# Second attention of a two-layer network: scores on one half of TensorE's rows, row maxima on the other, weighings in halves of 256 columns

## The reference, cut to what matters

```
q = (x @ Wq.T + bq).reshape(B, N, H, d)      # B=1, N=2048, H=16, d=8; k and v likewise
q, k = _rope(q, k)
scores = einsum('bhnd,bhmd->bhnm', q, k) / sqrt(d)
attn = softmax(scores, axis=-1)              # over 2048 keys, no mask
out = einsum('bhnm,bhmd->bhnd', attn, v)
return out.reshape(B, N, H*d) @ Wo.T + bo
```

## Time and profile before

| | us |
|---|---|
| median of 3 runs | 1331.21 (1330.64 to 1332.17) |
| the profiled execution | 1332.31 |
| its span | 1330.5 |
| first to last weighing tile of the second attention | 545.38 to 1219.41 of the span |
| TensorE busy | 1273.1 (96%) |
| VectorE busy | 955.4 (72%) |
| ScalarE busy | 861.5 (65%) |

### The profile page before, as it was taken

One profiled execution on the slowest core, in us unless ns is written; L12 is line 12 of the kernel. 1 busy time (PEld: TensorE's weight loads), 2 busy tenths in 40 slices (PEclk: granted clock), 3 DMA queues, 4 the chain that ended last, 5 costly groups with the idle time before them and its releaser, 6 DMA issues. The chain is left out here.

```text
span 1330.5 us, 22445 instructions
## 1 busy us (share of the span) xinstructions
PE 1273.1 (96%) x8134; PEld 729.4 (55%) x8134; DVE 955.4 (72%) x1664; ACT 861.5 (65%) x2406; POOL 189.8 (14%) x369
## 2 busy tenths in 40 slices
PE   5999999999988879999999999999999999999899
PEld 3677777777856643444444444444444444434577
DVE  4566666666667879888988889888888888846300
ACT  2566666666746420677777778777877778786442
POOL 3233333333453130000000000010000000000200
PEclk8999999999998975799999999999999999999899
DMA  2100000000000030000000000000000000000100
GB/s 79 71 10 1 9 10 10 9 1 4 1 1 0 1 148 27 17 20 21 21 22 22 7 16 21 22 16 7 21 21 22 4 19 4 6 5 1 36 17 16
DMA packets 21931, 25.58 MB, mean 19 GB/s; under 512 B 6277, under 2 KB 16293, under 8 KB 20582
## 3 DMA queue, kind: packets, MB, share of 16 engines
q1 hardware_dynamic: 21822, 24.15, 5.9%
HBM read 16.47 MB, written 5.24 MB: 16 GB/s over the span
## 5 line engine op out<-in xcount | busy, mean ns | idle before, releaser
L1206 DVE TENSOR_REDUCE rowmax<-psum 128x1 f32<-128x1024 f32 x512 | 602.8, 1219 | 86.6 <-PE psum L1076 86.4
L1311 ACT ACTIVATE pb<-psum 128x512 f32<-128x512 f32 x1024 | 531.9, 603 | 123.4 <-PE psum L1113 120.5
L1113 PE MATMUL psum<-qf,kf 64*128 64x512 f32 x1024 | 374.1, 441 | 1.6 <-ACT pb L1311 0.9
L1076 PE MATMUL psum<-kf,qf 64*128 64x512 f32 x1024 | 363.3, 454 | 6.3 <-DVE rowmax L1206 3.9
L1113 PEld LDWEIGHTS psum<-qf,kf 64*128 64x128 f32 x1024 | 171.1, 185 | 273.5 <-ACT pb L1311 253.1
L1101 PE MATMUL psum<-pb,vx 128*32 128x512 f32 x2048 | 273.6, 606 | 0.0
L1076 PEld LDWEIGHTS psum<-kf,qf 64*128 64x128 f32 x1024 | 166.4, 195 | 57.4 <-DVE rowmax L1206 31.5
L532 ACT ACTIVATE pr<-psum,nmax 128x128 f32<-128x128 f32 x256 | 93.9, 367 | 113.9 <-DVE nmax L475 113.8
L570 POOL TENSOR_TENSOR pr<-pr,rtotal 128x256 f32<-128x256 f32 (+1 forms) x256 | 110.5, 453 | 239.1 <-DVE rtotal L483 239.1
L474 DVE TENSOR_REDUCE nmax<-psum 128x2 f32<-128x256 f32 x128 | 53.7, 419 | 65.0 <-PE psum L343 65.0
L1345 POOL CAST nparts<-nfull 128x16 fp32r<-128x16 f32 x16 | 3.2, 197 | 665.2 <-DVE nfull L1215 665.2
(11 more groups left out here) (216 smaller groups left out, 1384.9 us busy)
## 6 DMA issues: line engine op xcount, KB each, us to landing
qf<-q_parts SPq DMA_DIRECT2D x30, 128.0 KB
kf<-k_parts SPq DMA_DIRECT2D x30, 128.0 KB
k_parts<-parts SPq DMA_DIRECT2D x4, 512.0 KB, 3.0
q_parts<-parts SPq DMA_DIRECT2D x4, 512.0 KB, 4.2
cos<-cos_table SPq DMA_DIRECT2D x1, 1024.0 KB
sin<-sin_table SPq DMA_DIRECT2D x1, 1024.0 KB
sumsT<-acc SPq DMA_DIRECT2D x60, 16.0 KB
attT<-acc SPq DMA_DIRECT2D x60, 16.0 KB
```

The lines of the kernel that those rows point to most:

```text
L1076: mm = nc.tensor.matmul(m.psum[:, M_B + (u % 2) * 2 + n % 2, :], qf[g0:g0 + HALFP, b, t * P:(t + 1) * P], kf[g0:g0 + HALFP, b, c * BANK:(c ...
L1113: nc.tensor.matmul(m.psum[:, bank, :], kf[g0:g0 + HALFP, b, t * P:(t + 1) * P], qf[g0:g0 + HALFP, b, c * BANK:(c + 1) * BANK], start=True, ...
L1206: nc.vector.tensor_reduce(rowmax[:, g % 2, u // 2, u % 2:u % 2 + 1], m.psum[:, M_B + (u % 2) * 2:M_B + (u % 2) * 2 + 2, :].rearrange("p b ...
L1311: nc.scalar.activation(pb[:, s % 3, c, :], m.psum[:, bank_of[(s, c)], :], ACT.Exp, scale=SCALE).then_inc(exp_ready, 1)
```

## The change

Scores are always on partitions 0-63, rows always on 64-127 (in the first loads too), so every head is loaded twice, once for each use: `load_rows` runs three heads ahead and `load_scores` two. Each half has its own two slots and its own semaphores. The clearing DMA is gone. The weighing of a tile is cut into two halves of 256 columns (four products each, 8 instructions on TensorE), the first after S1, the second after R3. A step becomes S0 R0, R1 S1, W(cols 0-255), S2 R2, S3 R3, W(cols 256-511). ScalarE's `save_sums` moves from behind the second exponential of a head's second tile to behind its fourth. `keep_clock` is always on partitions 0-63 and writes bank 6.

```diff
@@ load_first
-        part = slice(j * PARTS * HD1, (j + 1) * PARTS * HD1)
+        part = slice(HALFP + j * PARTS * HD1, HALFP + (j + 1) * PARTS * HD1)
@@ attn1_block
+        HALF_B = BANK // 2
-        def group(h):
-            return h % 2 * HALFP
+        SCORES, ROWS = slice(0, HALFP), slice(HALFP, P)
         def slot(h):
-            return h // 2 % SLOTS
+            return h % SLOTS
@@ sync
-                if h >= 4:
-                    sp.dma_start(qf[g0 + QROWS:g0 + KROWS, b, :] ...)
+            def load_rows(h):
+                if h >= SLOTS:
+                    sp.wait_ge(rows_reduced, (h - SLOTS + 1) * HALVES)
+                load(h, ROWS, rows_loaded)
+            def load_scores(h):
+                if h >= SLOTS:
+                    sp.wait_ge(av_done, (h - SLOTS + 1) * NT)
+                load(h, SCORES, scores_loaded)
...
-            for h in range(1, 3):
-                load(h)
+            load_rows(1)
+            load_scores(0)
             max_rows(0)
-            load(3)
+            load_rows(2)
+            load_scores(1)
             for h in range(H1 - 1):
                 max_rows(h + 1)
-                if h + 4 < H1:
-                    sp.wait_ge(av_done, (h + 1) * NT)
-                    load(h + 4)
+                if h + 3 < H1:
+                    load_rows(h + 3)
+                if h + 2 < H1:
+                    load_scores(h + 2)
                 move_sums(h)
@@ tensor
-                mm = nc.tensor.matmul(..., qf[g0:g0 + HALFP, b, t * P:(t + 1) * P],
-                                      kf[g0:g0 + HALFP, b, c * BANK:(c + 1) * BANK], ...)
+                mm = nc.tensor.matmul(..., qf[ROWS, b, t * P:(t + 1) * P],
+                                      kf[ROWS, b, c * BANK:(c + 1) * BANK], ...)
+            def weigh(h, t, part):
+                if part == 0:
+                    pe.wait_ge(exp_ready, h * UNITS + (t + 1) * NC)
+                    if t == 0:
+                        if h >= 1:
+                            pe.wait_ge(acc_saved, h)
+                        pe.wait_ge(vx_ready, h + 1)
+                cols = slice(part * HALF_B, (part + 1) * HALF_B)
+                for c in range(NC):
+                    mm = nc.tensor.matmul(m.psum[c * VCOLS:(c + 1) * VCOLS, A_B, cols], vx[:, h % VB, t, :],
+                                          pb[:, (h * NT + t) % 3, c, cols], start=(t == 0 and part == 0),
+                                          stop=(t == NT - 1 and part == 1))
+                if part == 1:
+                    mm.then_inc(av_done, 1)
@@ step
                     if c == 1:
                         scores(c)
                         if s >= 2:
-                            weigh((s - 2) // NT, (s - 2) % NT)
+                            weigh((s - 2) // NT, (s - 2) % NT, 0)
                         if t == NT - 2 and h + 1 < H1:
                             turn_max(h + 1)
+                    if c == NC - 1 and s >= 2:
+                        weigh((s - 2) // NT, (s - 2) % NT, 1)
@@ scalar
-                    if c == 1 and t == 1 and h >= 1:
+                    if c == NC - 1 and t == 1 and h >= 1:
                         save_sums(h - 1)
```

More of the change, by code:

```diff
@@ L947, in attn1_block @@
         rlast = sb("rlast", [P, NT])
-        loaded = [sem(f"qk_loaded{b}") for b in range(2 * SLOTS)]
+        rows_loaded = [sem(f"rows_loaded{b}") for b in range(SLOTS)]
+        scores_loaded = [sem(f"scores_loaded{b}") for b in range(SLOTS)]
         vx_zeroed, vx_ready = sem("vx_zeroed"), sem("vx_ready")
@@ L986, in last_out @@
             return halves[:, FIRST_HALF[t // TPB] + t % TPB, :]
-        def group(h):
-            return h % 2 * HALFP
+        SCORES, ROWS = slice(0, HALFP), slice(HALFP, P)
         def slot(h):
-            return h // 2 % SLOTS
-        def load_count(h):
-            return (LOAD if h % 4 else 0) + (h // 4) * (LOAD + 16)
+            return h % SLOTS
         bank_of, freed_by = {}, {}
@@ L1016, in _, with load @@
         def _(sp):
-            def load(h):
-                g0, b = group(h), slot(h)
+            def load(h, half, loaded):
+                b = slot(h)
                 hd = slice(h * HD1, (h + 1) * HD1)
                 for j in range(PARTS):
-                    part = slice(g0 + j * PARTS * HD1, g0 + (j + 1) * PARTS * HD1)
+                    part = slice(half.start + j * PARTS * HD1, half.start + (j + 1) * PARTS * HD1)
                     q = m.q_parts[j, hd, :].rearrange("(o d) n -> o d n", o=1).broadcast_to([PARTS, HD1, N])
-                    sp.dma_start(qf[part, b, :].bitcast(F32), q).then_inc(loaded[h % 4], 16)
-                    sp.dma_start(kf[part, b, :].bitcast(F32), m.k_parts[:, hd, :]).then_inc(loaded[h % 4], 16)
-                if h >= 4:
-                    sp.dma_start(qf[g0 + QROWS:g0 + KROWS, b, :].bitcast(F32),
-                                 qf[g0 + KROWS:g0 + KROWS + PARTS, b, :].bitcast(F32)).then_inc(loaded[h % 4], 16)
+                    sp.dma_start(qf[part, b, :].bitcast(F32), q).then_inc(loaded[b], 16)
+                    sp.dma_start(kf[part, b, :].bitcast(F32), m.k_parts[:, hd, :]).then_inc(loaded[b], 16)
+            def load_rows(h):
[6 more added lines that the diff above has]
+                load(h, SCORES, scores_loaded)
             def max_rows(h):
-                g0, b = group(h), slot(h)
+                b = slot(h)
                 sp.wait_ge(nT_saved, h + 1)
                 for j in range(PARTS):
-                    sp.dma_start(qf[g0 + QROWS + j:g0 + QROWS + j + 1, b, :].bitcast(F32),
+                    sp.dma_start(qf[QROWS + j:QROWS + j + 1, b, :].bitcast(F32),
                                  nT[j * NT:(j + 1) * NT, :].bitcast(F32)).then_inc(max_rows_loaded, 16)
@@ L1066, in rows @@
                 t, c, u = n // NC, n % NC, n // 2
-                g0, b = group(g), slot(g)
+                b = slot(g)
                 if n == 0 and g == 0:
@@ L1072, in rows @@
                 if n == 0 and g:
-                    pe.wait_ge(loaded[g % 4], load_count(g))
+                    pe.wait_ge(rows_loaded[b], (g // SLOTS + b) * LOAD)
                 if n % 2 == 0 and g * HALVES + u >= 2:
                     pe.wait_ge(rows_reduced, g * HALVES + u - 1)
-                mm = nc.tensor.matmul(m.psum[:, M_B + (u % 2) * 2 + n % 2, :], qf[g0:g0 + HALFP, b, t * P:(t + 1) * P],
-                                      kf[g0:g0 + HALFP, b, c * BANK:(c + 1) * BANK], start=True, stop=True)
+                mm = nc.tensor.matmul(m.psum[:, M_B + (u % 2) * 2 + n % 2, :], qf[ROWS, b, t * P:(t + 1) * P],
+                                      kf[ROWS, b, c * BANK:(c + 1) * BANK], start=True, stop=True)
                 if n % 2:
@@ L1091, in turn_max @@
                 nc.tensor.transpose(m.psum[0:PARTS * NT, bank, 0:P], nparts[:, :].bitcast(F32), m.ident[:, :]).then_inc(nT_ready, 1)
[L1093 to L1099, removed]
-                for c in range(NC):
-                    mm = nc.tensor.matmul(m.psum[c * VCOLS:(c + 1) * VCOLS, A_B, :], vx[:, h % VB, t, :], pb[:, (h * NT + t) % 3, c, :],
-                                          start=(t == 0), stop=(t == NT - 1))
-                mm.then_inc(av_done, 1)
+            def weigh(h, t, part):
[6 more added lines that the diff above has]
+                cols = slice(part * HALF_B, (part + 1) * HALF_B)
+                for c in range(NC):
+                    mm = nc.tensor.matmul(m.psum[c * VCOLS:(c + 1) * VCOLS, A_B, cols], vx[:, h % VB, t, :],
[3 more added lines that the diff above has]
+                    mm.then_inc(av_done, 1)
             def step(s):
                 h, t = s // NT, s % NT
-                g0, b = group(h), slot(h)
+                b = slot(h)
                 if t == 0:
+                    pe.wait_ge(scores_loaded[b], (h // SLOTS + 1) * LOAD)
                     pe.wait_ge(max_rows_loaded, (h + 1) * 32)
@@ L1112, in scores @@
                     bank = free_bank((s, c))
-                    nc.tensor.matmul(m.psum[:, bank, :], kf[g0:g0 + HALFP, b, t * P:(t + 1) * P],
-                                     qf[g0:g0 + HALFP, b, c * BANK:(c + 1) * BANK], start=True, stop=True).then_inc(st_ready, 1)
+                    nc.tensor.matmul(m.psum[:, bank, :], kf[SCORES, b, t * P:(t + 1) * P],
+                                     qf[SCORES, b, c * BANK:(c + 1) * BANK], start=True, stop=True).then_inc(st_ready, 1)
                 for c in range(NC):
@@ L1170, in turn, with keep_clock @@
                     mm.then_inc(turned, 1)
[L1172 to L1176, removed]
+            def keep_clock():
+                nc.tensor.matmul(m.psum[:, A_B, :], m.fill[SCORES, 0:P], m.fill[SCORES, :], start=True, stop=True)
             for n in range(UNITS):
                 rows(0, n)
-                keep_clock(HALFP)
+                keep_clock()
             for n in range(LEAD):
@@ L1184, in _ @@
                 rows(1, n)
-                keep_clock(0)
+                keep_clock()
```

(6 more changed lines are left out.)

## The result

| | before | changed |
|---|---|---|
| median of 4 runs, us | 1331.56 (1330.64 to 1332.17) | 1298.32 (1297.73 to 1300.12) |
| ratio | | 0.9753 (0.9736 to 0.9770) |
| profiled execution, its span | 1332.31, 1330.5 | 1297.83, 1296.0 |
| first to last weighing | 545.38 to 1219.41: 674.0 | 543.21 to 1184.88: 641.7 |

Faster by 33.2 us, where 36.6 was forecast; in the stage itself, from the first weighing to the last, it is 32.4 of the profiled execution. The page after answers to the earlier trace rows: TensorE does the same products with a quarter more instructions (10182 for 8134) in less time.

A forecast was written before the change was run, and what follows sets the result against it. A loop of S2, exponential, S1 and weighing was taken to bound the steps. 626.1 for steps, 4.4 first, 3.2 transposes and 3.7 saves gave 637.4 us, 36.6 less: 1294.6; 8 in 10 range 1268 to 1320.

The forecast's parts named there:

- What bounds it before: Second attention's common steps: a loop of S2, exponential, next S1 and weighing makes 2.60 us; TensorE waits 0.48 of it.
- The split weighing's price: Each step's two half weighings: 0.571 us each, so a step of 2.46 us, 0.35 above the floor of 2.12.
- Are there waits left: Inside the new step: no TensorE waits for exponentials (least slack 0.38 us) or reductions (slack 0.4); the loop is gone.
- The sides: Last three steps of a head: 12 serial pairs gone; alone, two long steps fall to 2.60, 13 us over 15 heads.
- Transposed maxima: Transpose of the maxima in each head: 0.21 us as before, 15 times, 3.2 us together.
- Save of the sums: ScalarE's copy of the sums delays a head's next weighing from 3.12 to 3.37: 0.25 us, 15 times, 3.7 together.
- Transposed maxima, the DMA: Maxima's way to the next head's score: 2.56 us from issue, there at 4.5, wanted at 5.1, slack 0.6.
- Nothing outside changes: Rest of the kernel, outside first to last weighing: same time, so the 36.6 us saved there is the whole gain.
- A: Rival, common steps: mode changes hide more than the rows say, VectorE bounds at 2.30 to 2.38; 1253 to 1273; 12%.
- C: Rival, half weighings: second pass's weight loads no longer covered, 0.215 us more each, step 2.89, 1404, slower; 7%.
- B: Rival, common steps: waits remain as a late pair delays the next, step 2.53 to 2.60, 1311 to 1329; 12%.
- D: Rival, last three steps: array halves bring nothing, pairs stay serial, 3.4 us a step, 1335; with the rest 2%.

## Why the prediction was right, and where it was off

The forecast was 1294.6, measured 1298.3; the term it rested on, the step, was exact, and its mechanism is what the trace shows. Little of the nearness is luck: two smaller errors at the ends of the stage, 0.6 and -1.2 us, go against each other.

- *What bounds it before*: the loop of S2, exponential, S1 and the weighing. Confirmed from both sides: with whole weighings, or both halves in one place, the step is 2.60 whatever the sides; with halves apart it is gone, also with the old sides.
- *The split weighing's price*: 0.571 forecast for a half, 0.57 measured; step 2.465 forecast, 2.466 measured. The line between the 128 and 512 column rows held, and quarters at full clock fit the same two numbers (0.36 forecast, 0.355).
- *Are there waits left*: none in a common step. ScalarE's exponentials and VectorE's reductions were ready in time, with VectorE at 92%.
- *The sides*: forecast 13 us alone, 12.4 measured; it was 0.88 over 15 heads, and serial pairs stand in 14: 12.3.
- *Transposed maxima*, too small: 0.21 taken from the step before, 0.27 measured, because the maxima take a place in the ring of three banks: the second pair behind the transpose has to wait for an exponential that ends at 896.67 (its weight load starts at 896.72, 0.29 behind the first pair's instead of 0.11), and the next half comes 0.38 behind it instead of 0.33. 0.9 us in all.
- *Save of the sums*, too small: 0.25 forecast, 0.31 measured: 0.9 us.
- *Transposed maxima, the DMA*: the term that failed. I gave it 2.56 us and a slack of 0.6, from one row. Landing is 2.47 in half of the heads and 2.9 to 3.9 in those where a fetch of instructions falls on it; that is 3.1 us in the profiled execution, which the forecast had at nothing. The kernel before has such a landing too (3.3 us, in the head whose maxima go at 751.74), but there the score was due late enough.
- *Nothing outside changes*: true of the code, not of the clock. Around 410 us, two stages before the changed code, the clock was at 0.70 in one profiled execution and at 0.80 in the other (the same window, before and after), and the stage began 1.3 us earlier; with the first steps it is 2.2 us that the profiled execution after has less.

```profile
402.00:419.00 17.00, 14.16 (x66) 9.84 (x65) 10.30 (x36) 11.95 (x18) 7.92 (x4) 0.70 0.00 0
```
```profile
402.00:419.00 17.00, 13.97 (x75) 9.71 (x75) 11.59 (x42) 12.86 (x19) 7.84 (x4) 0.80 0.00 0
```

Sum: 637.4 forecast from first to last weighing, 641.7 measured, 4.3 more. Of it 0.9 + 0.9 + 3.1 = 4.9 are named above. The first two steps took 4.32 and 3.10, where I had 4.4 and 2.47, since the second began at the low clock too: 0.6 more. The last two distances are shorter than a step, as they already were before (3.73 together), because no scores stand between the last weighings: 3.75 instead of 4.93, 1.2 less, which the sum had overlooked.

Of the rivals, A (changes partly hidden) and C (uncovered weight loads) are out by the step and by the quarters, whose 128-column passes are shorter than the loads' 0.16 and still cost what the line says. The step of 2.53 to 2.60 that B asked for did not come. D is out: the 12 pairs run side by side.

## What to carry to other kernels

A long block that feeds nobody, between two stages that feed each other over few buffers, closes a loop; cut it and spread it, and price each cut from the trace (here 0.35 us for each further way into and out of another tile size). Where there are buffers enough, don't cut: in the last head it cost about 5 us. Whether a whole weighing at another place in the step would break the loop too was not tested. Before adding up two edits, ask whether each removes the wait that hides the other's cost: here 12.4 and -2.6, each alone, made 33 together.

## What the runs showed of the hardware

- With the weighing in quarters, so four changes of tile size a step instead of two, TensorE is busy without a gap and yet stays at 0.50 of its clock if it was at 0.50 when that began: 5.23 us a step. Begun at 1.00 it stays there, at 3.14, as long as rows run beside scores; in the last head it fell in the execution that was traced. The split in halves rose from 0.60 in the first 5 us to 1.00 and stayed. Quarters from the start made the kernel 54% longer (1994.8 us against 1297.6); their price at full clock, 254 x 0.674 = 171 us, would have been 13%.
- A fetch of instructions (16 KB, in some cases 8 KB) that falls on a small DMA delays its landing by up to 1.4 us (2.47 to 3.9), and by 1.8 in one run (4.27, transpose earlier and last head whole). Where it falls is not fixed and changes with the code: the kernel before has one such landing with a fetch on it in 16, the changed one eight, and the one with the last tile whole a single one, of 2.95.
